# Two attention layers and two feed-forward layers in one kernel: the ternary weights' thirds ahead of the output copies, preparation in steps of two, the row update ahead of the second gate

## The reference

```python
x = x + L0_xattn(layernorm(x), ctx, masks, Wq, bq, Wk, bk, Wv, bv, Wo, bo)   # 32 heads of 16, 8 key groups, masked softmax
x = x + L0_ffn(layernorm(x), w1, g1, w2, g2, w3, g3)                          # ternary weights
x = x + L1_xattn(layernorm(x), ctx, ctx, gamma)                               # 8 heads over the sequence axis
x = x + L1_ffn(layernorm(x), w_gate_up, w_down)                               # silu(gate) * up, 2048 wide

# L0_ffn:
s  = mean(abs(w));  wq = round(tanh(w / (s + 1e-8))) * arctanh(s)
xq = round(rms(x) * g * scale) / scale, with scale = 127 / max|.| of the row
h  = silu(xq @ wq1.T) * (xq @ wq2.T);  out = quantised(rms(h) * g3) @ wq3.T
```

## Time and profile before

| | |
|---|---|
| median of 3 runs | 1550.69 us (1550.03 to 1552.88) |
| the profiled execution | 1555.64 us |
| its span, first to last instruction | 1553.9 us |
| mean granted TensorE clock | 0.955 |
| busy: TensorE, VectorE, ScalarE, GpSimd | 1392.8, 807.5, 728.9, 483.9 us |
| masked attention ends, ternary part begins | about 477 us |
| ternary part ends | about 716 us |

### The profile page before, as it was taken

How to read it: one execution, slowest core, us unless ns; L and a number is a source line. 1 busy time by engine, 2 the same in 40 slices (tenths; PEclk the granted TensorE clock), 3 DMA queues, 4 the chain that set the end, 5 groups by cost and what they waited for, 6 DMA issues and landing times. The chain is left out here.

```text
span 1553.9 us, 22502 instructions
## 1 busy us (share of the span) xinstructions
PE 1392.8 (90%) x8434; PEld 668.3 (43%) x8434; DVE 807.5 (52%) x1312; ACT 728.9 (47%) x1364; POOL 483.9 (31%) x522
## 2 busy tenths in 40 slices
PE   5678888788877989997899999989999999999998
PEld 4355655555533545552222222234444444444443
DVE  8864675566655778756666666525513211321220
ACT  3266666666665777772555565553501211210210
POOL 7211110356667676773222322144600000000000
PEclk9689999989989999997899999999999999999999
DMA  6646564746442001112644444233502002001000
GB/s 174 142 154 159 128 160 143 176 96 157 125 130 82 28 28 35 49 64 87 182 126 124 123 138 113 85 100 104 162 1 82 1 1 81 0 0 54 0 1 27
DMA packets 89447, 140.68 MB, mean 91 GB/s; under 512 B 8409, under 2 KB 47897, under 8 KB 88801
## 3 DMA queue, kind: packets, MB, share of 16 engines
q1 hardware_dynamic: 76544, 114.16, 27.0%
q10 hardware_dynamic: 12800, 25.17, 5.1%
HBM read 105.85 MB, written 33.46 MB: 90 GB/s over the span
## 5 line engine op out<-in xcount | busy, mean ns | idle before, releaser
L1792 DVE TENSOR_REDUCE c_negmax<-c_psA 128x1 f32<-128x512 f32 x256 | 165.9, 682 | 93.2 <-PE c_psA L1867 89.0
L2078 ACT ACTIVATE d_silu<-d_psGU 128x512 f32<-128x512 f32 x64 | 38.2, 596 | 344.7 <-PE d_psGU L2145 344.6
L2145 PE MATMUL d_psGU<-d_zt_hi,d_w_hi 128*128 128x512 bf16 x512 | 194.6, 380 | 4.0 <-ACT d_silu L2078 2.6
L2145 PE MATMUL d_psGU<-d_zt_lo,d_w_hi 128*128 128x512 bf16 x512 | 194.8, 381 | 0.0
L2145 PE MATMUL d_psGU<-d_zt_hi,d_w_lo 128*128 128x512 bf16 x512 | 194.8, 380 | 0.0
L1747 ACT ACTIVATE c_probs<-c_psB 128x512 f32<-128x512 f32 x256 | 140.4, 595 | 103.3 <-PE c_psB L1880 103.3
L894 DVE TENSOR_REDUCE a_negmax<-a_psX 128x4 f32<-128x1024 f32 x128 | 151.4, 1216 | 27.1 <-PE a_psX L1163 26.6
L2108 DVE TENSOR_TENSOR d_h<-d_psGU,d_silu 128x512 f32<-128x512 f32 x64 | 44.2, 691 | 223.7 <-PE d_psGU L2145 223.3
L753 ACT ACTIVATE a_probs<-a_psB 128x512 f32<-128x512 f32 x256 | 138.0, 592 | 18.8 <-PE a_psB L1175 18.2
L1867 PE MATMUL c_psA<-c_ks,c_qs 96*128 96x512 bf16 x256 | 104.0, 409 | 17.7 <-DVE c_negmax L1792 8.3
L1175 PE MATMUL a_psB<-a_qs,a_ks 115*128 115x256 bf16 x512 | 88.6, 292 | 33.4 <-ACT a_probs L753 31.4
(11 more groups left out here) (231 smaller groups left out, 2560.7 us busy)
## 6 DMA issues: line engine op xcount, KB each, us to landing
a_tern_stage<-in_w ACTq DMA_DIRECT2D x32, 768.0 KB, 5.8
d_weight_stage<-in_w_last SPq DMA_DIRECT2D x24, 512.0 KB, 4.2
a_ks<-k_scr SPq DMA_DIRECT2D x8, 768.0 KB
a_qs<-q_scr SPq DMA_DIRECT2D x8, 768.0 KB
c_ks<-k_scr SPq DMA_DIRECT2D x48, 128.0 KB, 2.6
c_qs<-q_scr SPq DMA_DIRECT2D x48, 128.0 KB, 3.0
a_xz<-in_x SPq DMA_DIRECT2D x32, 128.0 KB, 3.0
a_ctx<-in_ctx_t SPq DMA_DIRECT2D x8, 512.0 KB, 4.8
```

Of the source, the lines that this page charges most:

```text
L1792: v.tensor_reduce(negm[:, u:u + 1], A[:, u % 2, :], AX.X, ALU.max, negate=True)\
L2145: last = pe.matmul(GU[:, 2 * up + i % 2, :], wgu[wh][:, i, up, k, :], zt[zh][:, k, :], start=(k == 0 and j == 0), stop=(k == DC - 1 and j ...
```

## The change

Three things change. First, in masked attention ScalarE does all thirds of a group in one run behind both calls of `exponentials` and ahead of `results`; the normalisation of group 6 and the two logarithms of pass 4 stand ahead of `results` as well, and `THIRDS` has other numbers with the same sum. Second, in pass 7 VectorE's preparing goes on in groups 1 to 6, two of its twelve steps in each. Third, in the ternary part VectorE's update stands ahead of the second gate, its `take` of the x chunk behind the third gate and ahead of two reductions, and TensorE does the x transposes of a tile ahead of the first down product.

```diff
-    THIRDS = (0, 2, 4, 1, 2, 1, 2, 0)
+    THIRDS = (0, 3, 3, 2, 1, 2, 1, 0)
@@ ScalarE, attend(b), group g
-                    if g > 1:
-                        for k in behind[:1]:
-                            third(*k)
                     if to < BATCH:
                         exponentials(to, e + 1)
                     if n is not None and g == 0:
                         keys_high(n)
                     if n is not None and g == 1:
                         queries_high(n, 1)
+                    if b == TOTAL_AT and g == 1:
+                        act.wait_ge(s["total"], 4)
+                        act.activation(sc[:, 4, :], sc[:, 2, :], ACT.Ln).then_inc(s["total"], 1)
+                        act.activation(sc[:, 5, :], sc[:, 3, :], ACT.Ln).then_inc(s["total"], 1)
+
+                    for k in behind:
+                        third(*k)
+                    if g == 6 and b + 3 < BATCH:
+                        normalise(b + 3)
                     results(b, g)
                     if g == 0 and b:
                         out_high(b - 1, DC - 1)
                     if g in (2, 4, 6):
                         out_high(b, g // 2 - 1)
-                    if b == TOTAL_AT and g == 1:
...
-                    for k in behind[1 if g > 1 else 0:]:
-                        third(*k)
                     if b + 1 == BATCH and g >= GROUPS - 2:
                         front.rounded(act, g - GROUPS + 2)
-                    if g == 6 and b + 3 < BATCH:
-                        normalise(b + 3)
@@ VectorE, masked attention
+            def ahead():
+                for t in range(front.EARLY):
+                    yield from front.prepare(dve, t)
...
+                preparing = ahead()
...
-                    if b + 1 == BATCH and 1 <= g <= front.EARLY:
-                        for _part in front.prepare(dve, g - 1):
+                    if b + 1 == BATCH and 1 <= g <= 6:
+                        for _part in islice(preparing, 2):
                             pass
@@ VectorE, ternary part, tile t
                 next(ahead, None)
+                if t >= 3:
+                    update(t - 3)
                 if now:
                     gate(t, 1)
-                if t >= 3:
-                    update(t - 3)
                 take("h", t - 2, 1)
                 next(ahead, None)
                 if now:
                     gate(t, 2)
+                take("x", t + 1, 1)
                 next(ahead, None)
                 if now:
                     largest(t, 0)
-                take("x", t + 1, 1)
-                if now:
                     gate(t, 3)
@@ TensorE, ternary part, step n of tile t
-                    down(t - 3, n + 2) if n < 2 else down(t - 2, n - 2)
                     if n == 2:
                         for j in range(2):
                             transposed("x", t + 1, j)
+                    down(t - 3, n + 2) if n < 2 else down(t - 2, n - 2)
                     transposed("h", t - 2, n)
```

More of the change, by code:

```diff
@@ L786, in attend @@
                         out_high(b, g // 2 - 1)
-                    if b == TOTAL_AT and g == 1:
-                        act.wait_ge(s["total"], 4)
-                        act.activation(sc[:, 4, :], sc[:, 2, :], ACT.Ln).then_inc(s["total"], 1)
-                        act.activation(sc[:, 5, :], sc[:, 3, :], ACT.Ln).then_inc(s["total"], 1)
-                    for k in behind[1 if g > 1 else 0:]:
-                        third(*k)
                     if b + 1 == BATCH and g >= GROUPS - 2:
                         front.rounded(act, g - GROUPS + 2)
-                    if g == 6 and b + 3 < BATCH:
-                        normalise(b + 3)
             split_weight(0)
```

## The result

| | before | changed |
|---|---|---|
| median of 4 runs each, us | 1551.79 | 1526.20 |
| lowest to highest, us | 1550.03 to 1554.32 | 1523.77 to 1527.88 |
| the profiled execution, us | 1555.64 | 1523.77 |
| its last copy of output sums (end of masked attention), us | 466.59 | 438.04 |
| its last row update (end of the ternary part), us | 715.06 | 685.22 |

The ratio is 0.9833, with a 95% interval of 0.9812 to 0.9853: 25.6 us less. The forecast was 1520, range 1507 to 1543. By the two profiled executions masked attention gave 28.55 us, the ternary part 1.3 (from the last copy to the last update it was 248.47 us and is 247.18), and what lies behind, where nothing was changed, 2.0. The forecast had 22 and 9.

The account below looks back on a forecast made before the run. TensorE was taken to set the end, waiting for ScalarE's exponentials, VectorE's maxima and low halves, and the row update. 1555.64 - 22 (masked attention) - 9 (ternary part) = 1524.6; less 4.95 is 1519.7, so 1520 us, range 1507 to 1543.

Parts of the forecast that it names:

- Thirds ahead of the copy: Masked attention, Part 1: ScalarE's thirds move into its idle time before the copies; sum 23 us saved.
- The replay of pass 3: Masked attention, pass 3: 3.3 us saved by group 4 and 1.44 us in group 6, 4.7 us together.
- The replay of all passes: Masked attention: 23 us from the thirds plus 4.5 from short steps in pass 7, 27.5 us saved.
- the four fifths: Masked attention: 27.5 us cut to 22, bounds 0 and 32, because replays leave out small new waits.
- The third's load waits: Masked attention, ScalarE: waits of thirds for weight loads were to fall from 25.3 us to under 10.
- The rule of the Trainium skill that I set against the change: Masked attention loads: ScalarE's and SyncE's transfers share 16 engines, so earlier issue need not land earlier; priced in the slower rival.
- The rival that all low stretches go: TensorE's clock stays high once waits go, 15 us come back and not 5: 1510 us, chance 0.06.
- Short steps in pass 7: Masked attention, Part 2: VectorE prepares in steps of two; low half 2.5 us earlier, load wait 2 gone, 4.5 together.
- the loop: Ternary part, gate to gate over VectorE, GpSimd and ScalarE: 28.4 us for two tiles falls to 26.9.
- the ternary order brings nothing: Rival for the ternary part: gates are late by GpSimd's chain anyway, 1529 us, chance 0.12.
- Both signs of being wrong: TensorE comes to wait for the copies of the sums; the ternary part's pair of tiles stays at 28 us.
- Part 3: Ternary part: update and x transposes moved ahead; about 9 us saved, bounds 0 and 17.

Follow-up runs that it names:

- the eight profiles: Profiles of the eight runs with exactly the changed kernel's masked attention; last copy of the sums at 435.92 to 442.33 us.
- e1: Kernel before plus only the masked attention edits, ternary part as before: ratio to before 0.9856.
- e8: Changed kernel with the old table of thirds (0, 2, 4, 1, 2, 1, 2, 0) in the new places: ratio to before 0.9862.
- the second profile: The changed kernel itself, unaltered, measured once more: ratio to before 0.9816.
- e6: Changed kernel with ScalarE's last square of a tile issued behind the first silu of the next: ratio to before 0.9802.
- e10: Changed kernel with the take and transposes of x put back, the update still ahead of the second gate: ratio to before 0.9838.
- e11: Changed kernel with the update back behind the second gate, the take and transposes of x still ahead: ratio to before 0.9829.
- e5: Changed kernel with VectorE's product for the tile two ahead issued before the second gate, behind the update: ratio to before 0.9776.
- e2: Kernel before plus only the ternary part's edits, masked attention as before: ratio to before 0.9980.

## Why the prediction was right

**Thirds ahead of the copy: right, and its sum too small.** The replay of pass 3 said 4.7 us; the pass went from 51.4 to 46.3 (46.3 to 48.0 in the eight profiles). The replay of all passes, with the short steps, said 27.5 us. The eight profiles have their last copy at 439.1 us on the mean, 27.4 below that of before; by the medians e1 gives 24.4. So the last step, the four fifths, was off: 22 was too small, by 2 to 5 us, though e1's interval (18.2 to 26.5) still holds it. The step was to pay for small new waits. They came: 2.6 us more for low halves and 4.5 for the copies, beside the maxima's 6.1, which the replay had counted with 6.3. But of the 3.2 us for exponentials that were to stay in passes 0 and 4 only 0.5 did, and TensorE's own busy time fell by 9.9 us where 5 had been counted: 2.7 and 4.9 against 7.1.

**The loads.** The third's load waits fell to 16.3 us and not to under 10: a forecast that failed. Much of it lies in time in which the copy would have waited, but not all: it is one of the two things that spread the last copy over 6.4 us. The rule of the Trainium skill that I set against the change ("DMA: Bandwidth & Descriptors", section "Issuing engines are not separate DMA queues") agrees with e8, where the pieces that ScalarE issues beside SyncE's key and query rows land after 15.2 to 15.8 us in place of 4.6 to 5.6. It also fits the spread, though not with the key and query rows that the prediction named: those are loaded at the end of a pass. What stands ahead of the late pieces is the rows of x and of the context, and no run here changes these alone, so for the spread it isn't shown.

**The clock.** It is 0.95 in the stretch and was 0.93, so a part of the low stretches went. The rival that all low stretches go has not come true: the granted clock would be 1. The waits for maxima of up to 1.5 us stayed, as its counter-argument said, and after some of them the matmuls still run at the lower level.

**Short steps in pass 7: right as far as the profiles can tell,** 4.3 us for 4.5 with the thirds in place, 2.3 without. Behind the gains' wait of 6.9 us, which stayed, the low half's wait is 1.4 us and was 2.87.

**The ternary part: wrong.** The forecast had 9 us; by the marks it gave 1.3 (2.5 in the second profile), by the medians 2. The step that failed is the loop, 28.4 less the update (0.66) less "a wait for TensorE that was late (0.82): 26.9". Of its two subtractions one was never there to be had. The row named TensorE's V product as what ended the wait; but in the trace of before the product ends at 589.70 and ScalarE's silu, behind a square, at 589.88, 0.1 us before the gate. In the changed kernel the product was over 2 us before the gate and the silu 0.1 us; e6 takes the wait away by moving the square. The other was right and was eaten up: VectorE's product for the later tile moved into GpSimd's multiplication and grew by what the update had left. e10 and e11 show it: with the update in the loop the product takes 1.41 us, with the update ahead 2.08, and the pair is 28.1 to 28.2 either way. e5 takes the product out of the way. With both mended the pair is 26.71, so the forecast of 26.3 to 27 describes a kernel two edits away from this one. The rival "the ternary order brings nothing" had the right size for that part, within the 2.2 us that e2 can't tell from none, and the right reason, a loop over other engines; against it I had set that TensorE waits for the update alone, and e10 and e11 show that this is no argument.

**The total.** On the trace the terms made 31 us (1524.6 for the profiled execution), and the profiled execution came at 1523.77: that is luck, a term too small and one too large, and 2.0 us from a part that nothing had changed. By the medians, 31 us were forecast and 25.6 came: 2.4 more from masked attention than forecast, and about 7 less from the ternary part. The 6.2 us between 1520 and the median of 1526.2 are the step from the trace to the median: 4.95 was taken off, as the first profile lay that far above, and the second lay 2.4 below.

**The signs.** Of what was to show it, TensorE's waits for exponentials (under 12; 0.5), and those for maxima (20; 20.0) came as said, and the gains' wait stayed; the low half's wait is halved and not gone; ScalarE's idle before the copies fell further than said (25; 16.2), and the load waits (under 10; 16.3) and the pair (26.3 to 27; 28.22) did not come. Both signs of being wrong came: TensorE waits for the copies, 5.0 us, and the pair stays at 28. The first is small beside the 31 us that went; the second is the ternary part's failure.

## What to carry to other kernels

A wait shows who is late, not what sets the pace: where a part repeats, add up the loop from an instruction to itself over all engines, and ask of each wait in it which of its semaphores would come next if the named one were early. Work that one engine does in bursts belongs in front of the instruction that must wait anyway, with its loads asked for a whole gap earlier, and not beside other large loads. Where whole executions spread by more than an edit is worth, compare the profiles over the few groups that the edit touches: there the spread is small enough to tell. A move on VectorE is also a move against GpSimd: look at what GpSimd does in the place where a product with two operands in SBUF is to stand.

## What the hardware showed

VectorE's product of 128x1024 takes 1.27 us alone. Begun while GpSimd multiplies 128x512, it took 2.07 us with 0.99 us of GpSimd's work left (555.90 against an end at 556.89), and 2.24 us with 1.15 left (568.43, 569.58). That is the rest of GpSimd's instruction plus its own time, less 0.2: by these rows it waits, and does not share. The other way about, GpSimd's short steps wait for it: 1.62 us for a step of 0.56, 1.08 for one of 0.23. The Trainium skill states it ("SBUF — State Buffer", section "Who interferes with whom"): a VectorE instruction with two SBUF inputs and a GpSimd instruction that reads SBUF take the same read interface, and whichever comes second is blocked until the other has ended. The traces agree, but for the 0.2 us. By that rule, had the new place of the product been held against GpSimd's row, 0.67 us would have come back in the prediction's Part 3: a pair of 27.6 in place of 26.9, an estimate; with the wait of 0.82 for the silu, which stayed too, 28.4, against 28.2 measured.

ScalarE's load of a piece of 768 KB lands 15.2 to 15.8 us after its issue when SyncE starts the key and query rows at the same time (e8), and 4.6 to 5.6 us after it when it is issued 4.7 us ahead of them (the changed kernel).
